# Attention scores on four row tiles: three one-pass products of rounded and rest parts in place of one plain fp32 product

## What is computed

```
q = split_heads(x @ Wq + bq)          # 16 heads of 16
k = split_heads(ctx @ Wk + bk)        # ctx is x itself in SELF
v = split_heads(ctx @ Wv + bv)
s = einsum('bqhd,bkhd->bhqk', q, k) * 0.25
p = softmax(where(mask, s, min))      # causal mask in SELF, key mask in L0
h = einsum('bhqk,bkhd->bqhd', p, v) @ Wo + bo
x = layernorm(h + x)                  # or residual with the norm ahead of it
```

## Time and profile before

| | |
|---|---|
| median of 3 runs | 1485.25 us (1483.57 to 1486.38) |
| the profiled execution | 1486.97 us, span 1484.5 us |
| TensorE busy | 1444.9 us, 15592 matmul records |
| VectorE, ScalarE, GpSimd busy | 869.9, 782.0, 476.0 us |
| granted clock, mean | 0.994 of 2.4 GHz |

### The profile page before, as it was taken

One profiled execution on the slowest core, in us unless ns is written; L12 is line 12 of the kernel. 1 busy time (PEld: TensorE's weight loads), 2 busy tenths in 40 slices (PEclk: granted clock), 3 DMA queues, 4 the chain that ended last, 5 costly groups with the idle time before them and its releaser, 6 DMA issues.

```text
span 1484.5 us, 36270 instructions
## 1 busy us (share of the span) xinstructions
PE 1444.9 (97%) x15592; PEld 1137.0 (77%) x15592; DVE 869.9 (59%) x1639; ACT 782.0 (53%) x1305; POOL 476.0 (32%) x511
## 2 busy tenths in 40 slices
PE   5999999999999999999999999999998999999998
PEld 4777777777777777777777777777998999777775
DVE  2565656566666655455545656556697665555544
ACT  1656555555655555555565565565332333665663
POOL 6122123343443533332333311112477454110000
PEclk8999999999999999999999999999999999999999
DMA  7110100100000100000000100000000000000000
GB/s 286 36 43 23 36 22 8 51 8 15 8 8 8 44 2 1 2 2 2 2 2 23 37 8 9 15 8 22 25 6 4 11 2 1 15 29 29 29 16 29
DMA packets 13975, 34.40 MB, mean 23 GB/s; under 512 B 2167, under 2 KB 7543, under 8 KB 12407
## 3 DMA queue, kind: packets, MB, share of 16 engines
q1 hardware_dynamic: 13815, 32.09, 6.4%
HBM read 27.89 MB, written 4.19 MB: 22 GB/s over the span
## 4 chain that ended last, share of the span: by engine, by line
PE 90%; DVE 4%; ACT 2%; DMA 2%; issue 1%; SPq 0%; DVEq 0%; ACTq 0%
PE ps L639 11%; PE ps L702 10%; PE ps L537 10%; PE ps L666 8%; PE ps L587 7%; PE ps L715 6%; PE ps L560 5%; PE ps L683 5%; PE ps L548 5%; PE ps L728 5%; PE ps L644 3%; PE ps L693 3%; PE ps L527 2%; PE ps L607 2%; PE ps L663 2%; ACT s_PU L814 2%
## 5 line engine op out<-in xcount | busy, mean ns | idle before, releaser
L923 DVE TENSOR_REDUCE s_nm<-ps 128x8 fp32r<-128x960 f32 (+1 forms) x352 | 394.3, 1165 | 175.0 <-PE ps L587 129.9
L816 ACT ACTIVATE s_PU<-ps 120x1024 f32<-120x1024 f32 (+1 forms) x288 | 272.9, 1029 | 73.8 <-PE ps L644 73.7
L1062 POOL TENSOR_TENSOR s_xs<-s_xs,s_rowv 128x512 f32<-128x512 f32 x96 | 122.4, 1275 | 323.9 <-DVE s_nt L882 308.1
L825 ACT ACTIVATE s_Os<-ps 128x512 f32<-128x512 f32 x160 | 95.3, 598 | 216.1 <-PE ps L666 191.8
L639 PE MATMUL ps<-s_Qs,s_Kz 32*120 32x256 f32 (+2 forms) x3072 | 200.7, 374 | 2.1 <-DVE s_On L935 1.8
L537 PE MATMUL ps<-s_xT,s_W 128*128 128x256 f32 x640 | 159.2, 392 | 7.6 <-DMA s_xT<-x_t 7.0
L639 PEld LDWEIGHTS ps<-s_Qs,s_Kz 32*120 32x120 f32 (+1 forms) x3072 | 134.3, 180 | 33.2 <-issue 20.4
L1079 POOL TENSOR_SCALAR s_rs<-s_mv 128x2 f32<-128x2 f32 x96 | 21.1, 220 | 431.2 <-DVE s_mv L960 426.7
L702 PE MATMUL ps<-s_W,s_oT 128*128 128x256 f32 x640 | 156.8, 388 | 1.5 <-ACT s_oT L832 1.1
L778 ACT ACTIVATE s_Qs<-ps,s_colv 128x256 f32<-128x256 f32 x160 | 67.2, 472 | 163.0 <-PE ps L537 162.9
L537 PEld LDWEIGHTS ps<-s_xT,s_W 128*128 128x128 f32 x640 | 116.7, 192 | 41.0 <-ACT s_Os L825 17.7
(11 more groups left out here) (86 smaller groups left out, 2239.3 us busy)
## 6 DMA issues: line engine op xcount, KB each, us to landing
s_cT<-ctx_t SPq DMA_DIRECT2D x32, 240.0 KB, 2.6
s_W<-w_att SPq DMA_DIRECT2D x5, 1024.0 KB, 5.1
s_xs<-x_nat SPq DMA_DIRECT2D x4, 1024.0 KB, 12.0
s_xT<-x_t SPq DMA_DIRECT2D x16, 256.0 KB, 2.6
out<-s_xs SPq DMA_DIRECT2D x16, 256.0 KB, 2.0
s_rowv<-rows SPq DMA_DIRECT2D x6, 512.0 KB, 4.2
s_W<-w_ff SPq DMA_DIRECT2D x2, 1024.0 KB, 4.9
s_mi<-mask SPq DMA_DIRECT2D x8, 120.0 KB, 3.2
```

The costliest lines, as they stand in the source:

```text
L816: t = e.activation(P_of(i, k)[0:n, :, :], pair("B", i, k)[0:n, :, :], ACT.Exp, scale=0.25)
L825: e.activation(o[:, :, :].rearrange("p a n -> p (a n)"), bankM("PV", i, hf), ACT.Copy).then_inc(sem["PVe"])
L923: e.tensor_reduce(o, v, AX.X, ALU.max, negate=True).then_inc(sem["max"])
L1062: e.tensor_tensor(xs[:, b, :, :], xs[:, b, :, :], row2(layer, 0), ALU.add).then_inc(sem["pool"])
```

## The change

Q and K are split as FFN's operands are, and each plain product of A and B becomes three products of f32r tiles, in the order of PARTS. For this:

- Qe becomes Qh on ScalarE (writes the rounded part) and Ql on VectorE (accumulator + bias - rounded part = rest). The bank of Q is free after Ql.
- Ke becomes Kh on ScalarE and Kl on VectorE, which write a tile Kf (one slot) without the zeroed heads, and Kx on GpSimd: four multiplications by hsel, two of the rounded part after Kh and two of the rest after Kl. A waits for Ql and Kx. The bank of K is free after Kl.
- The zeroed key tiles and FFN's hidden tiles share one ring KH of two slots, since the split tiles need twice the room. Qs is twice as large.
- pickr shrinks from 128 stored columns to one, which the matmul reads again and again.
- The key bias is no longer stored in two zeroed copies (20 columns of constants in place of 30).
- All due times (WANT), the costs of A and B in LONG and STAY are other numbers, so the order of stages on every engine can differ.

```diff
--- before
+++ after
-STAY = 0.464
+STAY = 0.439
...
-        self.ring = {"Q": Slots(3), "Kz": Slots(2), "PU": Slots(7), "Vp": Slots(2), "cT": Slots(2),
+        self.ring = {"Q": Slots(3), "KH": Slots(2), "Kf": Slots(1), "PU": Slots(7), "Vp": Slots(2), "cT": Slots(2),
                      "xT": Slots(2), "nt": Slots(2), "Os": Slots(3), "On": Slots(2), "oT": Slots(2), "nm": Slots(2), "mT": Slots(2),
...
-                           ("H", (i, u), [("F2", i, u)])])
+                           ("KH", ("H", i, u), [("F2", i, u)])])
...
-                rings=[("MI", ("Q", i, 0), [("Qe", i, 0)]), ("Q", i, [("B", i, u) for u in range(units(i))])])
-            add("ACT", "Qe", after=[("Q", i, 0)])
+                rings=[("MI", ("Q", i, 0), [("Ql", i, 0)]), ("Q", i, [("B", i, u) for u in range(units(i))])])
+            add("ACT", "Qh", after=[("Q", i, 0)])
+            add("DVE", "Ql", after=[("Qh", i, 0)])
...
-                    rings=[("MI", ("K", i, 0), [("Ke", i, 0)]), ("Kz", i, [("B", x, u) for x in key_users(i) for u in range(units(i))])])
-                add("ACT", "Ke", after=[("K", i, 0)])
+                    rings=[("MI", ("K", i, 0), [("Kl", i, 0)]), ("Kf", i, [("Kx", i, 0)]),
+                           ("KH", ("K", i), [("B", x, u) for x in key_users(i) for u in range(units(i))])])
+                add("ACT", "Kh", after=[("K", i, 0)])
+                add("DVE", "Kl", after=[("Kh", i, 0)])
+                add("POOL", "Kx", after=[("Kl", i, 0)])
...
-                add("PE", "A", u, after=[("Qe", i, 0), ("Ke", first, 0)] + ([("mf", first, 0)] if layer == "L0" else []),
+                add("PE", "A", u, after=[("Ql", i, 0), ("Kx", first, 0)] + ([("mf", first, 0)] if layer == "L0" else []),
                     rings=[("S", ("A", i, 2 * u + q), [("max", i, 2 * u + q)]) for q in range(2)]
-                    long=(1.75 if not u else 1.32) if self_ else .93 if layer == "L0" else None)
+                    long=(1.76 if not u else 1.27) if self_ else .78 if layer == "L0" else None)
...
-        Qs = [sb(f"Qs{i}", [128, 2, S]) for i in range(3)]
-        Kz = [sb(f"Kz{i}", [128, 2, 2, 256]) for i in range(2)]
+        Qs = [sb(f"Qs{i}", [128, 2, 2, S], f32r) for i in range(3)]
+        Kf = [sb(f"Kf{i}", [128, 2, 2, 256], f32r) for i in range(1)]
+        KH = [sb(f"KH{i}", [128, 2, 4, 256], f32r) for i in range(2)]
...
-        Hs = [sb(f"Hs{i}", [128, 2, 4, S], f32r) for i in range(2)]
...
-        pickr = sb("pickr", [128, 4, 128], f32r)
+        pickr = sb("pickr", [128, 4], f32r)
...
-                        for j in range(4):
-                            if g == 0 and j == 2:
-                                empty("A", i, 2 * u + 1)
-                            t = e.matmul(banks[j][:, 240 * g:240 * g + 240].rearrange("p (c n) -> p c n", c=2),
-                                         q[row[j], g, 128 * u:128 * u + 128], kz[row[j], g, :, c0:c0 + C],
-                                         start=(g == 0 and layer != "L0"), stop=(g == 1))
+                        for x, (lq, lk) in enumerate(PARTS):
+                            for j in range(4):
+                                if g == 0 and x == 0 and j == 2:
+                                    empty("A", i, 2 * u + 1)
+                                t = e.matmul(banks[j][:, 240 * g:240 * g + 240].rearrange("p (c n) -> p c n", c=2),
+                                             q[row[j], lq, g, 128 * u:128 * u + 128], kz[row[j], lk, g, :, c0:c0 + C],
+                                             start=(g == 0 and x == 0 and layer != "L0"), stop=(g == 1 and x == 2))
...
-                    for j in range(4):
-                        if x == 0 and j == 2:
-                            empty("B", i, 2 * u + 1)
-                        e.matmul(banks[j][0:n, wide * x:wide * x + wide], kz[row[j], g, c, k0:k0 + n], q[row[j], g, qs_],
-                                 start=(x == 0), stop=False)
+                    for y_, (lq, lk) in enumerate(PARTS):
+                        for j in range(4):
+                            if x == 0 and y_ == 0 and j == 2:
+                                empty("B", i, 2 * u + 1)
+                            e.matmul(banks[j][0:n, wide * x:wide * x + wide], kz[row[j], lk, g, c, k0:k0 + n], q[row[j], lq, g, qs_],
+                                     start=(x == 0 and y_ == 0), stop=False)
                 w.wait_ge(sem["mTe"], nth("mTe", i))
                 for x, (g, c, k0, qs_) in enumerate(parts):
                     for j in range(4):
-                        t = e.matmul(banks[j][0:n, wide * x:wide * x + wide], pickr[row[j], 2 * g + c, 0:n], mt[row[j], qs_],
+                        t = e.matmul(banks[j][0:n, wide * x:wide * x + wide], pickr[row[j], 2 * g + c:2 * g + c + 1].to_broadcast([32, n]), mt[row[j], qs_],
                                      start=False, stop=(x == len(parts) - 1))
                 t.then_inc(sem["B"])
...
-            def Qe(i):
+            def Qhi(i):
...
                 for g in range(2):
-                    t = e.activation(Q_of(i)[:, g, :], m[:, g * 256:g * 256 + 256], ACT.Identity, bias=bq(layer_of(i), g))
+                    t = e.activation(Q_of(i)[:, 0, g, :], m[:, g * 256:g * 256 + 256], ACT.Identity, bias=bq(layer_of(i), g))
...
-            def Ke(i):
+            def Khi(i):
...
-                for c in range(2):
-                    for g in range(2):
-                        t = e.activation(K_of(i)[:, g, c, :], m[:, g * 256:g * 256 + n], ACT.Identity, bias=bk(layer_of(i), c, g),
-                                         scale=hsel[:, c:c + 1])
-                t.then_inc(sem["Ke"])
+                for g in range(2):
+                    t = e.activation(Kf_of(i)[:, 0, g, :], m[:, g * 256:g * 256 + n], ACT.Identity, bias=bk(layer_of(i), g))
+                t.then_inc(sem["Kh"])
...
-                if was is not None:
-                    w.wait_ge(sem["F2"], nth("F2", *was))
+                h, v = H_of(i, u), pair("F1", i, u)
+                was = ring["KH"].before["H", i, u]
+                if was[0] == "H":
+                    w.wait_ge(sem["F2"], nth("F2", was[1], was[2]))
+                else:
+                    w.wait_ge(sem["B"], max(nth("B", x, v_) for x in key_users(was[1]) for v_ in range(units(was[1]))))
                 w.wait_ge(sem["F1"], nth("F1", i, u))
...
+            def Qlo(i):
+                m, q = bankM("Q", i), Q_of(i)
+                w.wait_ge(sem["Qh"], nth("Qh", i))
+                for g in range(2):
+                    t = e.scalar_tensor_tensor(q[:, 1, g, :], m[:, g * 256:g * 256 + 256], bq(layer_of(i), g), q[:, 0, g, :].bitcast(f32),
+                                               ALU.add, ALU.subtract)
+                t.then_inc(sem["Ql"])
+
+            def Klo(i):
+                m, n, kf = bankM("K", i), keys(i), Kf_of(i)
+                w.wait_ge(sem["Kh"], nth("Kh", i))
+                for g in range(2):
+                    t = e.scalar_tensor_tensor(kf[:, 1, g, :], m[:, g * 256:g * 256 + n], bk(layer_of(i), g), kf[:, 0, g, :].bitcast(f32),
+                                               ALU.add, ALU.subtract)
+                t.then_inc(sem["Kl"])
...
+            def Kx(i):
+                kf, kz, was = Kf_of(i), K_of(i), ring["KH"].before["K", i]
+                if was is not None and was[0] == "H":
+                    w.wait_ge(sem["F2"], nth("F2", was[1], was[2]))
+                elif was is not None:
+                    w.wait_ge(sem["B"], max(nth("B", x, u) for x in key_users(was[1]) for u in range(units(was[1]))))
+                w.wait_ge(sem["d_cst"], N_CST)
+                for part in range(2):
+                    w.wait_ge(*((sem["Kl"], nth("Kl", i)) if part else (sem["Kh"], nth("Kh", i))))
+                    for c in range(2):
+                        behind()
+                        e.tensor_scalar(kz[:, part, :, c, :], kf[:, part, :, :].bitcast(f32), hsel[:, c:c + 1], None,
+                                        ALU.mult).then_inc(sem["pool"])
```

More of the change, by code:

```diff
@@ L448, in Q_of, with Kf_of, K_of, H_of @@
         def Q_of(i): return Qs[slot("Q", i)]
-        def K_of(i): return Kz[slot("Kz", keys_first(i))][:, :, :, 0:keys(i)]
+        def Kf_of(i): return Kf[slot("Kf", i)][:, :, :, 0:keys(i)]
+        def K_of(i):
+            return KH[slot("KH", ("K", keys_first(i)))].rearrange("p l (g c) n -> p l g c n", c=2)[:, :, :, :, 0:keys(i)]
+        def H_of(i, u): return KH[slot("KH", ("H", i, u))]
         def P_of(i, k): return PU[slot("PU", ("P", i, k))]
@@ L594, in A @@
                     for g in range(2):
-                        for j in range(4):
-                            if g == 0 and j == 2:
-                                empty("A", i, 1)
-                            e.matmul(banks[j][:, 256 * g:256 * g + 256].rearrange("p (c n) -> p c n", c=2), q[row[j], g, 0:128],
-                                     kz[row[j], g, :, 0:128], start=(g == 0), stop=False)
```

(44 more changed lines are left out.)

63 lines of the change are left out of this document (26 added, 37 removed).

## The result

The changed kernel takes **1516.62 us** (median of 4 runs, 1515.82 to 1519.73) against 1485.62 us (4 runs) for the kernel before: ratio 1.0215, 95% interval [1.0197, 1.0233]. The prediction said 1454 us and gave slower 5 in 100. The time lies 43 us above the top of the range. The profiled execution has a span of 1515.3 us.

A forecast was written before the change was run, and what follows sets the result against it. TensorE was taken to bound the kernel: 39.2 us saved on products minus 8 of losses gave net 31, so 1456 from the profiled 1486.97, and 1454 us for the median; range 1438 to 1474.

The forecast's parts named there:

- Quad prices, and the sum of 39.2: A and B on TensorE: one-pass quads of 256 columns cost 0.12 us; summed over stages, 39.2 us less.
- Rival 3: A and B: loading and issuing three weights per product sets the pace, mean quad above 0.138; 1620 us at 0.20; chance 0.04.
- rival 1: A and B: quads go at pure column time, 64 us less on TensorE, 1430 us; chance 0.07.
- A microsecond of array time taken away is a microsecond of the end.: TensorE, busy 1444.9 of 1484.5 us: its savings reach the end fully while new work on other engines stays hidden.
- One input, so I take the lower: GpSimd's four multiplications per key tile: 0.64 us each, between rows of 0.635 and 1.275; 122 us in all, at most 245.
- Both hold, so I cost this at nothing inside a layer.: Longer key and query chains before A in L1: covered by 11.4 and 5.4 us of slack, so no cost.
- Nothing in the change leaves the array idle long enough to expect another: TensorE's granted clock: stays at 1.00 of 2.4 GHz, with no loss priced.
- Start at 1 us: First batch, a chain with nothing beside it: the longer chain costs 1 us.
- The borders at 2.5 each: Two FFN borders, where hidden tiles share two slots with the keys: 2.5 us lost on each.
- The new order may have more or fewer turns ... 2 us, left for the range.: Turns between row tiles and whole array on TensorE, 0.21 us each: ten either way are 2 us.
- Making the split, 8 us of loss in all.: Losses around the products: 1 first batch, 1 last batch, 5 FFN borders, 1 new small stalls, 8 us together.
- Rival 2: Waits on VectorE, GpSimd and shared slots return most of the gain: about 1473 us, up to 1485; chance 0.15.

The follow-up runs named there:

- products_alone: Kernel before in its own order, each plain A and B product made three f32r products with zeros for the rests: 1464.25 us, ratio 0.9852.
- kx_narrow: Changed kernel in its own order, GpSimd's key multiplications cut to 16 columns after the first use of each slot: 1486.26 us, ratio 1.0001 to the kernel before.
- products_replanned: products_alone with the planner's costs of A and B set to the changed kernel's, so the order is made anew: 1479.83 us, ratio 0.9955.
- kx_cost_planned: Changed kernel with only the planner's cost of a key tile on GpSimd raised from 2.6 to 6.2: 1497.7 us, ratio 1.0078 to the kernel before.
- pool_new_order: Changed kernel, multiplications still on GpSimd at planned cost 6.2, weights requested later, measured split-stage costs, due times searched anew: 1470.38 us, ratio 0.9897 to the kernel before.

## Why the prediction was wrong, step by step

**The sign is wrong, the range doesn't hold the time, and two steps failed; a third was too simple.** The time is 62.6 us above the forecast. Along the runs at the end of this section some 17 of them are products that bring 22 us and not 39, some 15.5 an order that was made anew, 30 GpSimd's instruction; the rest of the split and the shared slots took 6.4 where 8 were priced.

- *Quad prices, and the sum of 39.2.* Right in mechanism, a little high in size. Same order: 33.3 us off TensorE (products_alone); in the other order 36.8. Rival 3 (a slower quad) and rival 1 (column time, 0.108) both fell: 0.118 for 256 columns. The 512 ones come 0.231 apart, where 0.22 was taken. These distances alone don't explain the 6 us less; that stays open.
- *"A microsecond of array time taken away is a microsecond of the end."* Too simple. 33.3 gave 22, 36.8 gave 27, 171.5 gave 103. Idle time of TensorE in the same order went from 39.6 to 50.9 us. I take it that work of other engines that a longer score stage had covered now ends after it; no run separates this.
- *"One input, so I take the lower": 0.64 us for each multiplication.* **The first step that failed.** 1.485 and 1.567 us, above even the bound of 1.275: I chose between two rows by the number of inputs, and both were other operations than the one priced. With 0.368 us each, the changed kernel's order takes 1486 us instead of 1517 (kx_narrow). These 30 us are nearly the whole loss of 31 against the kernel before, but half of the miss of 62.6, and since 0.368 is below the 0.64 priced they are the most that this price can have cost. With every multiplication that short the time is still 12 us above the top of the range.
- *"Both hold, so I cost this at nothing inside a layer."* **The second.** I named what is queued behind GpSimd's multiplications, the inverse deviations among them, and then judged by the idle share and by the keys' own slack of 11.4 us. The keys indeed held, away from the L3 border. The inverse deviation had no such slack, and behind it stood ln, the maxima and M: 14.6 us of waiting on TensorE in six places, each up to 3.8 us. The signs of being wrong named only A's waits for keys and query remainders, so they would have missed it in steady L1.
- *"Nothing in the change leaves the array idle long enough to expect another" clock.* It did: 48 us at 1.2 GHz against 17, by the estimate above 12 us of TensorE time more. This was in no term.
- *Start at 1 us.* First A 15 us later; moving the weights back gives 5 of them, and 1 to 2 us of the end. What the late start costs by itself in the end stays open.
- *The borders at 2.5 each.* By themselves the shared slots cost 1 us. With multiplications of 1.5 us they cost a 7.1 us wait before L3.
- *"The new order may have more or fewer turns ... 2 us, left for the range."* The turns are 3 us. But the order is more than turns: with the same instructions it moved the time by 15.6 (products_replanned) and by 19 (kx_cost_planned). This was in no term and no bound.
- *Making the split, 8 us of loss in all.* 30 to 35 us when the order is made for it. Rival 2 was this mechanism and said 1473, up to 1485; it was too small, and it had no price for the order.

The loss adds up along a row of runs; with another sequence the shares would be others, as pool_new_order shows for GpSimd's. It is 1485.6 before, 1464.3 with the products, 1479.8 with their costs planned, 1480.9 with shared slots, 1483.6 with the split in short instructions and the changed kernel's own due times, 1486.3 with VectorE's at full length, 1516.6 with GpSimd's.

## What to carry to other kernels

Before pricing work moved onto an idle engine, list what stands behind it in that engine's order and ask what slack that has: the new work's own slack and the engine's idle share say nothing about it. A price between two rows of other operations goes to the dearer one, and past it for the range. Where a planner or a hand-made order depends on costs, a wrong cost can lose more than the instruction, and an experiment that changes only the order (same instructions) belongs beside every one that changes work. And give the kernel before the same new order: without that control the changed kernels would have looked 16 to 18 us faster than the kernel before, while the same treatment gives that one some 20. And add to a wait what the granted clock loses behind it.

## What the runs showed of the hardware

A GpSimd multiplication by a per-partition column takes 1.485 us for 480 elements and 0.368 for 32, so about 2.5 ns an element and 0.29 us fixed; the same on ScalarE takes 0.695, and GpSimd's two-input addition of 512 elements 1.275. On TensorE, one-pass quads of rounded operands come 0.118 us apart at 256 columns (median over B of the paired layers, kernel after) and 0.113 at 240. The second quad of such a B stage starts later, 0.216 behind the first. The timeline of products_alone shows four of the six quads of an A stage in CROSS, 240 columns: 0.21 to the second, then 0.10 to 0.12:

```profile
863.40 0.39 PE L590 MATMUL ps<-s_Kz,s_Qs 32*128 32x240 f32 x4
863.61 0.28 PE L590 MATMUL ps<-s_Z,s_Qs 32*128 32x240 f32 x4
863.73 0.28 PE L590 MATMUL ps<-s_Kz,s_Z 32*128 32x240 f32 x4
863.83 0.28 PE L590 MATMUL ps<-s_Kz,s_Qs 32*128 32x240 f32 x4
```

In L1 a wait of TensorE of 3.78 us was followed by a stretch at 1.2 GHz, and before L3 the clock fell to it within a wait of 7.14 us. At that level a one-pass quad of 240 columns took 0.24 us.
